# Long attention on one core: the key chunks of the first two query groups searched together

## The chip, the cores and the metric

The kernel runs on one core of one Trainium2 chip. The metric is the device time of one execution in microseconds (us); the figure for a kernel is the median over its runs.

## The reference, cut to what matters

The program is one long network over 2048 tokens of width 128. The order of its parts is a gated mixing block, two transformer layers with causal attention and experts (called `f` in the names of the trace), one attention without a mask (`b`), and the two transformer layers again (`g`). The change touches `b` alone:

```python
def _L0_attn_b_ref(x, Wq, bq, Wk, bk, Wv, bv, Wp):      # x: (1, 2048, 128)
    H, D = (16, 8)
    q = (x @ Wq + bq).reshape(Bb, Nn, H, D)
    ...
    q = jnp.einsum('bnhe,ei->bnhi', q, Wp)
    k = jnp.einsum('bnhe,ei->bnhi', k, Wp)
    scores = jnp.einsum('bnhi,bmhi->bnhm', q, k) / math.sqrt(D)
    attn = jax.nn.softmax(scores, axis=-1)
    out = jnp.einsum('bnhm,bmhe->bnhe', attn, v).reshape(Bb, Nn, E)
```

Every one of 2048 queries of 16 heads looks at all 2048 keys. The softmax is computed with the row maximum taken off first, and this maximum has to be found before the exponentials of a row can start.

## The kernel before, in words

**Tiling.** Tokens lie in 4 chunks (`CHUNKS`) of 512 and in 16 tiles of 128, 4 tiles to a chunk. Heads are taken 4 at a time (a quad). In `b` a *group* is one chunk of queries `c`, one quad and two of the chunk's four tiles, so 256 queries of 4 heads. There are 32 groups, in the order of `FULL_ORDER`: the 8 of query chunk 0 first. Groups 0 and 1 are the two halves of the same chunk and the same quad.

**Inputs.** Before `b`'s attention, `project_qkv` projects chunk by chunk. Queries and keys go out to DRAM in three bf16 parts and come back with another layout into `q_stack` and `k_stack`; each chunk of each stack is brought by DMAs of line 678, for the two halves of the partitions, on the SP, POOL and ACT queues. TensorE waits for a chunk of keys on its first use (`inputs("k", p)`).

**Search.** For each group, 16 *scans* (2 tiles, 2 pairs of heads, 4 chunks of keys) are searched: TensorE writes 128 queries times 512 keys of two heads into one of two buffers of `h_ps_scanb` (line 1393, two matmuls that run side by side), VectorE takes the maximum of 1024 columns (line 1545) and frees the buffer. `h_maxima_..b` holds the partial maxima, in two buffers by group number modulo 2. After a group's last scan VectorE reduces them to `h_row_maxb` (line 1564), TensorE turns that (`turn`, line 1413), VectorE negates it into `h_shiftsb` (line 1570), and SP sends it by DMA into a row of `q_stack` (line 1611), where it enters the scores as one more row of the product.

**Scores, exponentials, values.** For each group there are 16 *steps*, one per tile of keys. A step is one pair of score banks (line 1431, `h_ps_lowb` or `h_ps_highb`, a ring of 3), two exponentials on ScalarE (line 1497, `h_probsb`, a ring of 12), and 8 value matmuls (line 1452). After a group's last step ScalarE drains the result (`h_drainedb`, line 1506) and SP writes it out (line 1618).

**Order.** All three streams go through TensorE, which works in the order of its instructions. That order is fixed at build time by `Plan.orders()`: a loop that keeps modelled due times of each engine and picks the next of search, scores and values in turn, with some patience for the one whose turn it is. `Plan.searched` is the order of the search pieces. Two rules of the planner matter here: scores of a group may start only 4.2 us (`SHIFT`) after its turn, and a scan of group g may be placed only when the scoring has reached group g-2 (`x[1] - self.units[2 * n_pair][0] > 2` forbids it). The planner does not model the arrival of the key chunks. In `b` the search order is: the 16 scans of a group, tile by tile, pair by pair, and innermost the 4 chunks of keys; `turn` of a group stands behind the first scan of the next one.

After the last turn come the pieces `finish` (projection of the first three chunks of the result), placed in the same list.

Of the kernel before, what the change touches and what calls it, by code (L numbers as in the profile page):

```python
# [19 lines left out]
CHUNKS = S // CH  # L20
# [35 lines left out]
class Steps:  # L56


    def __init__(self, engine, sem, base=0):
        self.engine, self.sem, self.base, self.n = engine, sem, base, 0  # L60
# [973 lines left out]
SCALAR, SCALAR_NEXT, SCALAR_DONE = 0.833, 68.0, 222.0  # L1034
HIDE, SHIFT, WRITE = 85.0, 4200.0, 3000.0
INVERT, BIAS, SCALE, ADD, FINISH_COLUMNS = 450.0, 2200.0, 850.0, 1800.0, 4 * 650.0
INVERT_AFTER, GATHER, MOMENTS, KEEP = 5, 3500.0, 4500.0, 2200.0
CAUSAL_ORDER = [(c, n) for c, n in enumerate((TPC, TPC, 2, 2)) for _ in range(QUADS * TPC // n)]
FULL_ORDER = [(c, 2) for c in range(CHUNKS) for _ in range(QUADS * 2)]
# [4 lines left out]
class Plan:  # L1044
# [6 lines left out]
    def __init__(self, causal):  # L1051
        self.causal = causal
        if causal:
            chunks = CAUSAL_ORDER
        else:
            chunks = FULL_ORDER
        seen = [0] * CHUNKS
        self.groups = []
        for c, n in chunks:
            self.groups.append((c, seen[c] // TPC, seen[c] % TPC, n))  # L1060
            seen[c] += n
        assert seen == [QUADS * TPC] * CHUNKS
        self.blocks = [TPC * c + t0 + n if causal else TILES for c, _, t0, n in self.groups]
        self.searched = []
        for g, (c, _, t0, n) in enumerate(self.groups):
            pieces = [("scan", g, p, ((hp, t, SCAN_KEYS),)) for t in range(t0, t0 + n) for hp in range(2)
                      for p in range(c if causal else CHUNKS)]
            if causal:
                for hp in range(2):
                    pieces += [("scan", g, c, tuple((hp, t, (t + 1) * P) for t in ts)) for ts in self.together(g)]  # L1070
                if n == TPC:
                    pieces.append(("scan", g, c, ((0, 1, 2 * P), (1, 1, 2 * P))))
            self.searched += pieces[:1] + ([("turn", g - 1)] if g else []) + pieces[1:]
        self.searched.append(("turn", len(self.groups) - 1))
        self.searched += [("finish", c) for c in range(CHUNKS - 1)]
        if causal:
            self.searched += [("rows", c) for c in range(CHUNKS - 1)]
        self.ends = [max(g for g, x in enumerate(self.groups) if x[0] == c) for c in range(CHUNKS)]
        self.invert_at = {min(i for i, x in enumerate(self.searched) if x[:2] == ("scan", self.ends[c] + INVERT_AFTER)): c
                          for c in range(CHUNKS - 1)}  # L1080
        self.scale_at = self.searched.index(("finish", 0))
        self.turn_at = {x[1]: i for i, x in enumerate(self.searched) if x[0] == "turn"}
        self.end_of_search = {x[1]: i for i, x in enumerate(self.searched) if x[0] == "scan"}
        self.steps = [(g, kb) for g in range(len(self.groups)) for kb in range(self.blocks[g])]
        self.step_at = {x: n for n, x in enumerate(self.steps)}
        self.units = [(g, kb, k) for g, kb in self.steps for k in range(self.banks(g))]
        self.unit_at = {x: u for u, x in enumerate(self.units)}
        self.step_of = [self.step_at[x[0:2]] for x in self.units]
        self.exps = []
        for u, (g, kb, k) in enumerate(self.units):  # L1090
            self.exps.append(("exp", u))
            if g and (kb, k) == (0, self.banks(g) - 1):
                self.exps.append(("drain", g - 1))
        self.exps.append(("drain", len(self.groups) - 1))
        self.offsets = [max(0, kb - TPC * self.groups[g][0] - self.groups[g][2]) * P if causal else 0
                        for g, kb in self.steps]
        self.tensor, self.moves = self.orders()
# [1438 lines left out]
```

How the kernel before makes its waits and increments, by code:

```python
    def __call__(self, instruction):  # L62
        self.n += 1
        instruction.then_inc(self.sem, 1)
        self.engine.wait_ge(self.sem, self.base + self.n)
# [126 lines left out]
        @block.sync  # L192
# [16 lines left out]
                rest.append((m.w_att[:, :, i, :], ins["L0_ffn_" + name].rearrange("l p d -> p l d")))  # L209
            for i, name in enumerate(("Wq", "Wk", "Wv")):
                rest.append((m.w_b[:, i, :], ins["L0_attn_b_" + name]))
            for dst, name in ((m.bv[:, 0:LAYERS, :], "bv"), (m.bo[:, :, :], "bo"), (m.gate_b[:, :, :], "gate_b")):
                rest.append((dst, ins["L0_ffn_" + name].partition_broadcast(P)))
            rest.append((m.bv[:, LAYERS, :], ins["L0_attn_b_bv"].partition_broadcast(P)))
            rest.append((m.gate_w[:, :, :], ins["L0_ffn_gate_w"].rearrange("l p e -> p l e")))
            assert len(rest) == REST_LOADS
            for dst, src in rest:
                sp.dma_start(dst, src).then_inc(rest_in, 16)
            sp.wait_ge(rest_in, 16 * REST_LOADS)
            sp.wait_ge(x_in, 16)
# [1 line left out]
        @block.gpsimd  # L222
# [1 line left out]
            nc.gpsimd.memset(m.ident[:, :], 0.0).then_inc(built, 1)  # L224
            nc.gpsimd.memset(m.pick[:, :, :], 0.0).then_inc(built, 1)
            nc.gpsimd.memset(m.hide_right[:, :, :], 0.0).then_inc(built, 1)
            nc.gpsimd.memset(m.upto[:, :], 1.0).then_inc(built, 1)
            nc.gpsimd.memset(m.ones[:, :], 1.0).then_inc(built, 1)
            pool.wait_ge(built, 5)
            def select(t, op, fill, column, row, base=0):
```

## Time and profile before

| | us |
|---|---|
| median of 3 runs | 3134.47 (3134.13 to 3141.97) |
| profiled execution, its own time | 3133.52 |
| profiled execution, its span | 3131.5 |
| first scan of `b` (start) | 1316.6 |
| last drain of `b` (start) | 1975.0 |

The span is the stretch that the profiler saw; the time of the same execution is 2.0 us longer. Times in the rows are from the span's start. PE is the matrix engine, PEld its weight loads, DVE is VectorE, ACT ScalarE, POOL GpSimd, SP the queue of SyncE. "[1.03 <-PE x]" behind an instruction is the idle time of its engine just before it and what ended it. The granted clock (PEclk) is a share of 2.4 GHz: 1.00 is 2.4 GHz and 0.50 is 1.2 GHz.

### The profile page before, as it was taken

How to read it: one execution, taken by the hardware profiler on the slowest of the kernel's cores; microseconds unless marked ns; L12 is line 12 of the kernel's file. 1: busy time of each engine (PE TensorE's matmuls, PEld its weight loads, DVE VectorE, ACT ScalarE, POOL GpSimd, SP SyncE). 2: the span in 40 equal slices, each digit the busy share in tenths (PEclk: the TensorE clock that was granted, in tenths of full speed). 3: DMA queues.
4: the chain of work that ended last, by engine and by line, in shares of the span. 5: the costliest groups of instructions: out<-in, count | busy, mean ns of one | idle time of the engine just before them, and what ended most of it. 6: DMA issues, size and time to landing. Idle time of an engine off the chain costs nothing. (4 is left out here: it accounts for less than half of the span.)

```text
span 3131.5 us, 71460 instructions
## 1 busy us (share of the span) xinstructions
PE 2659.0 (85%) x28144; PEld 1161.8 (37%) x28144; DVE 2612.3 (83%) x3520; ACT 2248.4 (72%) x4330; POOL 608.7 (19%) x1145
## 2 busy tenths in 40 slices
PE   3569999899799995569999999489998998899976
PEld 3322333577323333312222223232333776323325
DVE  4569999787899995689999999389998887899976
ACT  1137988677489884349999998358887676688864
POOL 5233101444321011100000000132101443321011
PEclk8669999999899997879999999779999999899998
DMA  1061000215300000410000000330000215300001
GB/s 33 21 142 33 21 14 12 66 55 101 72 26 20 18 9 24 108 31 9 12 12 13 12 14 10 79 86 25 16 18 16 75 48 105 66 24 19 13 13 30
DMA packets 109882, 119.08 MB, mean 38 GB/s; under 512 B 20726, under 2 KB 87660, under 8 KB 109548
## 3 DMA queue, kind: packets, MB, share of 16 engines
q1 hardware_dynamic: 102444, 98.21, 12.0%
q0 software_dynamic: 4608, 13.96, 2.5%
q8 instruction: 222, 3.64, 0.5%
q10 hardware_dynamic: 2496, 2.36, 0.4%
q14 instruction: 112, 0.92, 0.1%
HBM read 70.31 MB, written 43.78 MB: 36 GB/s over the span
## 5 line engine op out<-in xcount | busy, mean ns | idle before, releaser
L1497 ACT ACTIVATE h_probsf<-h_ps_lowf 128x512 f32<-128x512 f32 (+3 forms) x812 | 424.3, 551 | 130.9 <-PE h_ps_lowf L1431 81.1
L1497 ACT ACTIVATE h_probsg<-h_ps_lowg 128x512 f32<-128x512 f32 (+3 forms) x812 | 424.3, 551 | 120.5 <-PE h_ps_lowg L1431 77.9
L1497 ACT ACTIVATE h_probsb<-h_ps_lowb 128x512 f32<-128x512 f32 x683 | 389.1, 596 | 78.6 <-PE h_ps_lowb L1431 60.4
L1452 PE MATMUL h_ps_valuesf<-h_probsf,v_all 128*9 128x256 f32 (+2 forms) x4608 | 353.6, 380 | 39.1 <-POOL h_probsf L1595 31.8
L1452 PE MATMUL h_ps_valuesg<-h_probsg,v_all 128*9 128x256 f32 (+2 forms) x4608 | 352.4, 378 | 30.3 <-POOL h_probsg L1595 22.9
L1452 PE MATMUL h_ps_valuesb<-h_probsb,v_all 128*9 128x256 f32 x4096 | 318.4, 383 | 9.3 <-ACT h_drainedb L1506 5.0
L1545 DVE TENSOR_REDUCE h_maxima_0b<-h_ps_scanb 128x2 f32<-128x1024 f32 x256 | 292.4, 1213 | 29.1 <-PE h_ps_scanb L1393 29.1
L1545 DVE TENSOR_REDUCE h_maxima_2b<-h_ps_scanb 128x2 f32<-128x1024 f32 x256 | 292.7, 1214 | 6.7 <-PE h_ps_scanb L1393 6.7
L1545 DVE TENSOR_REDUCE h_maxima_0f<-h_ps_scanf 128x2 f32<-128x1024 f32 x224 | 259.1, 1216 | 22.4 <-PE h_ps_scanf L1393 21.7
L1545 DVE TENSOR_REDUCE h_maxima_0g<-h_ps_scang 128x2 f32<-128x1024 f32 x224 | 258.9, 1215 | 19.8 <-PE h_ps_scang L1393 19.1
L1497 ACT ACTIVATE h_probsf<-h_ps_highf 128x512 f32<-128x512 f32 (+3 forms) x404 | 224.1, 555 | 37.2 <-PE h_ps_lowf L1431 34.6
L1497 ACT ACTIVATE h_probsg<-h_ps_highg 128x512 f32<-128x512 f32 (+3 forms) x404 | 224.1, 555 | 36.1 <-PE h_ps_lowg L1431 33.4
L1595 POOL TENSOR_SCALAR_AFFINE_SELECT h_probsg<-h_probsg 128x128 f32<-128x128 f32 (+1 forms) x384 | 125.6, 341 | 617.1 <-ACT h_probsg L1497 610.0
L1393 PE MATMUL h_ps_scanf<-k_stack,q_stack 48*128 48x512 bf16 (+3 forms) x1280 | 221.9, 367 | 26.6 <-issue 9.0
L1595 POOL TENSOR_SCALAR_AFFINE_SELECT h_probsf<-h_probsf 128x128 f32<-128x128 f32 (+1 forms) x384 | 124.9, 341 | 599.7 <-ACT h_probsf L1497 592.6
L1393 PE MATMUL h_ps_scang<-k_stack,q_stack 48*128 48x512 bf16 (+3 forms) x1280 | 219.1, 362 | 26.0 <-DVE h_maxima_0g L1545 7.7
L1431 PE MATMUL h_ps_lowf<-q_stack,k_stack 49*128 49x256 bf16 (+2 forms) x1368 | 229.6, 289 | 10.4 <-DMA q_stack<-h_shiftsf 4.5
L1431 PE MATMUL h_ps_lowg<-q_stack,k_stack 49*128 49x256 bf16 (+2 forms) x1368 | 227.7, 287 | 10.5 <-DMA q_stack<-h_shiftsg 4.3
L1393 PE MATMUL h_ps_scanb<-k_stack,q_stack 48*128 48x512 bf16 x1024 | 200.7, 389 | 39.6 <-DMA k_stack<-k_parts 25.5
L1497 ACT ACTIVATE h_probsb<-h_ps_highb 128x512 f32<-128x512 f32 x341 | 203.4, 596 | 18.6 <-PE h_ps_lowb L1431 15.5
L1431 PE MATMUL h_ps_lowb<-q_stack,k_stack 49*128 49x256 bf16 x1366 | 200.5, 275 | 10.3 <-ACT h_probsb L1497 10.1
L1545 DVE TENSOR_REDUCE h_maxima_2g<-h_ps_scang 128x2 f32<-128x1024 f32 x160 | 185.5, 1217 | 14.5 <-PE h_ps_scang L1393 13.5
(480 smaller groups left out, 5220.5 us busy)
## 6 DMA issues: line engine op xcount, KB each, us to landing
q_stack<-combine_weights SPq DMA_DIRECT2D x64, 256.0 KB, 3.6
q_stack<-in_L_ffn_e_w SPq DMA_DIRECT2D x24, 256.0 KB, 3.2
q_stack<-q_parts SPq DMA_DIRECT2D x22, 256.0 KB, 5.9
k_stack<-k_parts SPq DMA_DIRECT2D x22, 256.0 KB, 8.1
attended<-h_drainedf SPq DMA_DIRECT2D x16, 256.0 KB, 2.5
attended<-h_drainedf SPq DMA_DIRECT2D x32, 128.0 KB, 1.9
attended<-h_drainedb SPq DMA_DIRECT2D x32, 128.0 KB, 1.9
attended<-h_drainedg SPq DMA_DIRECT2D x16, 256.0 KB, 2.2
```

What stands on the lines that cost most here:

```text
L1393: last = nc.tensor.matmul(ps_scan[:, i % RING_A, b, at:at + width], m.q_stack[rows, c, 2 * quad + hp, t * P:(t + 1) * P], m.k_stack[rows, ...
L1431: last[b] = nc.tensor.matmul(ps_scores[(2 * n_pair + b) % RING_S][:, width * i + off:width * (i + 1)], m.k_stack[rows, kb // TPC, pair, at ...
L1452: last = nc.tensor.matmul(ps_values[32 * j:32 * j + VD, low:high], m.v_all[:, kb, QUAD * quad + j, :], probs[:, (u + j % banks) % RING_P, ...
L1497: nc.scalar.activation(by_head(probs[:, of % RING_P, :], of), by_head(ps_scores[of % RING_S], of), ACT.Exp, scale=SOFTMAX_SCALE).then_inc( ...
L1545: nc.vector.tensor_reduce(found[:, :, low], now, AXIS_X, ALU.max).then_inc(freed, 1)
L1595: nc.gpsimd.affine_select(out=at, in_=at, compare_op=ALU.is_ge, fill=0.0, base=0, pattern=[[0, at.shape[1]], [1, P]], channel_multiplier=- ...
```

## The change

The planner's order of search pieces is changed for the attention without a mask. The 32 scans of groups 0 and 1 form one list, sorted by chunk of keys: 4 scans of group 0 and 4 of group 1 with chunk 0, the same with chunk 1, chunk 2 and chunk 3. The turn of group 0 stands behind the first scan of group 1 with chunk 3, which is the 29th scan; the last three scans of group 1 follow. From group 2 on the order is the old one, so the turn of group 1 stands behind the first scan of group 2. Scans, turns, scores and values are the same in number and size; `orders()` is run on the new list, and so the interleaving of the three streams on TensorE follows from it.

```diff
+TOGETHER = 2
 ...
+            if not causal and g < TOGETHER:
+                first = sorted(first + pieces, key=lambda x: x[2]) if g else pieces
+                if g == TOGETHER - 1:
+                    at = next(i + 1 for i in range(len(first)) if first[i][1] == g and first[i][2] == CHUNKS - 1)
+                    self.searched += first[:at] + [("turn", 0)] + first[at:]
+                continue
             self.searched += pieces[:1] + ([("turn", g - 1)] if g else []) + pieces[1:]
```

## Rows read from the trace of the kernel before

**Rows 1.** The page: busy time, share of span and instructions of each engine.

```profile
span 3131.5 us, 71460 instructions
PE 2659.0 (85%) x28144; PEld 1161.8 (37%) x28144; DVE 2612.3 (83%) x3520; ACT 2248.4 (72%) x4330; POOL 608.7 (19%) x1145
```

**Rows 2.** Busy time by stretch of `b`: us, then PE, PEld, DVE, ACT, POOL, clock, DMA.

```profile
1316.00:1344.30 28.30, 2.20 (x10) 0.47 (x10) 3.85 (x4) 0.16 (x1) 4.40 (x8) 0.52 0.99 201
1344.30:1364.30 20.00, 10.35 (x39) 1.77 (x35) 19.39 (x19) 0.00 (x0) 0.00 (x0) 0.50 0.00 0
1364.30:1400.00 35.70, 34.69 (x398) 9.74 (x398) 33.75 (x33) 31.20 (x59) 0.00 (x0) 0.90 0.02 5
1400.00:1949.00 549.00, 525.30 (x6523) 155.25 (x6523) 538.74 (x525) 508.21 (x957) 0.00 (x0) 1.00 0.04 12
1949.00:1975.50 26.50, 22.90 (x269) 7.51 (x268) 6.76 (x19) 21.84 (x42) 0.00 (x0) 1.00 0.02 6
```

**Rows 3.** Timeline of DVE at the start of `b`: start, us, instruction, count.

```profile
1317.14 1.23 DVE L1545 TENSOR_REDUCE h_maxima_0b<-h_ps_scanb 128x2 f32<-128x1024 f32 x1 [0.97 <-PE h_ps_scanb L1393]
1323.67 1.23 DVE L1545 TENSOR_REDUCE h_maxima_0b<-h_ps_scanb 128x2 f32<-128x1024 f32 x1 [5.31 <-PE h_ps_scanb L1393]
1336.35 1.23 DVE L1545 TENSOR_REDUCE h_maxima_0b<-h_ps_scanb 128x2 f32<-128x1024 f32 x1 [11.45 <-PE h_ps_scanb L1393]
1344.35 14.80 DVE L1545 TENSOR_REDUCE h_maxima_0b<-h_ps_scanb 128x2 f32<-128x1024 f32 x13 [6.78 <-PE h_ps_scanb L1393]
1359.18 0.19 DVE L1564 TENSOR_REDUCE h_row_maxb<-h_maxima_0b 128x8 f32<-128x32 f32 x1
1359.29 1.22 DVE L1545 TENSOR_REDUCE h_maxima_2b<-h_ps_scanb 128x2 f32<-128x1024 f32 x1
1360.42 0.27 DVE L1570 TENSOR_SCALAR h_shiftsb<-h_ps_scanb 8x128 bf16<-8x128 f32 x1
1361.21 6.88 DVE L1545 TENSOR_REDUCE h_maxima_2b<-h_ps_scanb 128x2 f32<-128x1024 f32 x6 [0.53 <-PE h_ps_scanb L1393]
...
1372.12 8.01 DVE L1545 TENSOR_REDUCE h_maxima_2b<-h_ps_scanb 128x2 f32<-128x1024 f32 x7 [0.35 <-PE h_ps_scanb L1393]
1380.16 0.19 DVE L1564 TENSOR_REDUCE h_row_maxb<-h_maxima_2b 128x8 f32<-128x32 f32 x1
```

**Rows 4.** Who waited for whom from 1316 to 1344.35: total, times, longest.

```profile
PE h_ps_scanb L1393 <- DMA k_stack<-k_parts: 25.5, 3, 12.1
```

**Rows 5.** Timeline of ACT and PE where the first scores start.

```profile
1364.94 1.09 ACT L1497 ACTIVATE h_probsb<-h_ps_lowb 128x512 f32<-128x512 f32 x2 [48.78 <-PE h_ps_lowb L1431]
...
1364.30 0.61 PE L1431 MATMUL h_ps_lowb<-q_stack,k_stack 49*128 49x256 bf16 x4
...
1368.49 1.04 PE L1452 MATMUL h_ps_valuesb<-h_probsb,v_all 128*9 128x256 f32 x8
...
1370.43 1.04 PE L1452 MATMUL h_ps_valuesb<-h_probsb,v_all 128*9 128x256 f32 x8
...
1373.09 0.62 PE L1452 MATMUL h_ps_valuesb<-h_probsb,v_all 128*9 128x256 f32 x8
...
1374.18 0.62 PE L1452 MATMUL h_ps_valuesb<-h_probsb,v_all 128*9 128x256 f32 x8
```

**Rows 6.** Timeline around one change of group in the middle of `b`.

```profile
1706.32 0.39 PE L1393 MATMUL h_ps_scanb<-k_stack,q_stack 48*128 48x512 bf16 x2
1706.80 0.12 PEld L1452 LDWEIGHTS h_ps_valuesb<-h_probsb,v_all 128*9 128x9 f32 x8 [0.38 <-ACT h_probsb L1497]
1706.80 0.62 PE L1452 MATMUL h_ps_valuesb<-h_probsb,v_all 128*9 128x256 f32 x8
1707.35 0.11 PEld L1431 LDWEIGHTS h_ps_lowb<-q_stack,k_stack 49*128 49x128 bf16 x4 [0.43 <-DMA q_stack<-h_shiftsb]
...
1707.78 1.08 ACT L1497 ACTIVATE h_probsb<-h_ps_lowb 128x512 f32<-128x512 f32 x2 [1.03 <-PE h_ps_lowb L1431]
...
1708.43 0.28 PE L1431 MATMUL h_ps_highb<-q_stack,k_stack 49*128 49x256 bf16 x1 [0.47 <-ACT h_probsb L1497]
...
1708.75 0.39 ACT L1506 ACTIVATE h_drainedb<-h_ps_valuesb 128x256 f32<-128x256 f32 x1
1709.01 0.62 ACT L1497 ACTIVATE h_probsb<-h_ps_highb 128x512 f32<-128x512 f32 x1
```

**Rows 7.** Timeline of the end of `b`'s attention: last row maxima, last drain.

```profile
1948.43 0.19 DVE L1564 TENSOR_REDUCE h_row_maxb<-h_maxima_2b 128x8 f32<-128x32 f32 x1
...
1975.01 0.38 ACT L1506 ACTIVATE h_drainedb<-h_ps_valuesb 128x256 f32<-128x256 f32 x1 [0.74 <-PE h_ps_valuesb L1452]
```

## The prediction

> **What bounds the kernel now.** I read the busy shares first [rows 1]: no engine is full over the whole span, so the answer must come from the stage that the change touches. The chain of work that ended last goes back only to 1990.8 us and never reaches `b`'s attention, so it says nothing here. I therefore cut `b` into stretches [rows 2]. Four regimes are to be seen. From 1316 to 1344.3 every engine is idle (VectorE 3.85 us busy of 28.3) while the DMA engines are at 0.99: the stage waits for the key chunks. From 1344.3 to 1364.3 only the search runs, with VectorE at 19.39 of 20.00 us. From 1400 to 1949 all three engines are close to full, VectorE the fullest: 538.74 of 549.00 us, 98.1%, against 95.7% of TensorE and 92.6% of ScalarE. The last 26.5 us belong to the scores of the last group.
>
> The start in detail [rows 3]: VectorE does one scan of each key chunk at 1317.14, 1323.67, 1336.35 and 1344.35, with idle gaps of 5.31, 11.45 and 6.78 us before the last three, 23.54 us together. The waits name the cause: TensorE waited three times, 25.5 us in all, for DMAs of `k_stack` [rows 4]. After the fourth chunk has landed, 13 reductions run in 14.80 us. With one reduction alone at 1.23 us that is (14.80 - 1.23) / 12 = 1.131 us per scan.
>
> In the middle, one group takes VectorE (1948.43 - 1380.16) / 30 = 18.94 us from one row maximum to the next [rows 3, 7]: 16 scans are 18.1, the rest is the row maximum, the shift and the small gap at the turn. ScalarE and TensorE need less for a group's scores. A step takes 1.09 us (from 1373.09 to 1374.18 between two value blocks [rows 5]), so 16 steps are 17.44 us, and the drain adds 0.26 (from 1708.75 to 1709.01 [rows 6]): 17.7. The missing 1.2 us is visible once per group: TensorE does a scan and values at 1706.32 and 1706.80 with no scores between, ScalarE idles 1.03 us, and the scores start when the DMA of the shifts has landed [rows 6]. So before, the scores of every group wait for the search of that group, and the search is paced by VectorE. That is the path which sets the end of the stage; what is saved on VectorE ahead of the last turn is saved at the end, if nothing else takes over.
>
> **The change, part by part.** *Removed:* the idle time at the chunks. Eight scans need each chunk instead of one. Starting at 1317.14, VectorE is done with the 8 scans of chunk 0 at 1317.14 + 9.05 = 1326.2, after the first use of chunk 1 was possible (1323.67). The 16th is over at 1335.2; chunk 2 can be reduced at 1336.35, so 1.1 us of idle time stays. The 24th is over at 1345.4, after chunk 3 (1344.35), so no gap. Recovered: 23.54 - 1.1 = 22.4 us. The projections and the DMA issues ahead do not depend on the scans, so I keep the landing times.
>
> *Moved:* the row maximum of group 0 comes after 28 scans: 1336.35 + 12 x 1.131 + 0.1 = 1350.0, where before it came at 1359.18. One scan later stands its turn, at 1351.3. From the shift at 1360.42 to the first scores at 1364.30 there were 3.9 us [rows 3, 5], so the scores start at about 1355.2, 9.1 us earlier. The row maximum of group 1 comes at about 1355.6 instead of 1380.16, 24.5 us earlier. Behind each of these stand the same instructions as before: one turn on TensorE, one shift on VectorE, the DMAs of line 1611 on SP, with no wait in front of them on SP, since the first write of a result comes a whole group later. No instruction is added; the sort costs nothing on the chip.
>
> *The clock.* Scans alone do not bring TensorE to 2.4 GHz here: from 1344.3 to 1364.3 they ran at a granted 0.50, that is 1.2 GHz [rows 2], and steps took 1.94 us (1368.49 to 1370.43) until 1371.5, 7.2 us after the first scores [rows 5]. In that time VectorE lost about 1.9 us: 15 scans of group 1 took 18.92 us from 1361.21 to 1380.13 where 15 x 1.131 + 0.1 = 17.1 were due [rows 3]. I take the same loss in the new kernel, now in group 2: the 24.5 us are then 22.6, in keeping with the 22.4 above. The Trainium skill, page "TensorE: Matmul & The Clock Gate", Part 1, holds that the throttled clock is the default and that activity releases it; as the new kernel has no long gap on TensorE after 1317, that rule leaves room for a clock that stays up, while the rows here show 20 us of just such scans at 1.2 GHz. By the row the sum stays 22.4; by the rule the 1.9 us would come on top, 24.3.
>
> *The streams after that.* Now group 0 and group 1 are both searched when the first scores start, and the scores have a stock. Scores of group 1 could start at 1356.7 + 3.9 = 1360.6, and are reached only after 16 steps from 1355.2, with four of them slow: 1355.2 + 16 x 1.13 + 4 x 0.8 = 1376.5. So the scoring is 16 us behind what the search would allow, and the scores of a group no longer wait. They gain 18.94 - 17.7 = 1.2 us per group, and have caught up after 13 groups or so; with 31 to go, the last groups wait for their search as before, and the tail from the last row maximum to the last drain (1948.43 to 1975.39, 27 us [rows 7]) is unchanged. In code the same count shows: the search has 17 pieces per group (16 scans and the turn), the scores have 16, and a strict rotation lets them gain one step per group.
>
> *What this costs:* (a) the rule of two groups ahead. The first scan of group 3 may be placed only when the scores of group 1 have begun. The search is 50 pieces in at that point, the scores begin at about piece 33 and need 16: just met or missed by one round. Between 0 and 1.1 us (one scan), I take 0.5. For later groups the search loses one place per group against that bound, and it is met. (b) While the scores catch up, 17 steps fall on one group of search. ScalarE then needs 17 x 1.09 + 0.26 = 18.8 us of 18.94, so three engines run with almost no slack over rings of 2 and 3 buffers. No row of before shows this. From below: 0, as the engines fit. From above: TensorE's wait for ScalarE at a change of group, 0.47 us [rows 6], passed on to VectorE in each of 14 groups, 6.6 us. I take 0.5, near the lower end, since VectorE ran on through the same 0.47 us waits in the middle of `b`.
>
> *Sum:* 22.4 - 0.5 - 0.5 = 21.4 us. The profiled execution took 3133.52 us (span 3131.5), so 3112.1; the median of the runs shown is 1.0 us higher, so the forecast is 3113. After `b` all stages start earlier by the same amount and have the same work.
>
> **The rivals.** *The scores become the bound (gain 9).* They start only 9.1 us earlier. If in the crowded rotation a group of scores still takes 18.94 us, because TensorE's order or ScalarE's drain holds it, then they never catch up, and the stage ends 9.1 us earlier: 3125.4. For it: ScalarE would be 99% busy. Against it: the steps of 1.09 us in rows 5 ran with a scan in each of them. Its first mark is that the scores still trail by 10 us or more at the last group. Chance 0.09.
>
> *The clock stays at 2.4 GHz (gain 24).* The scans keep it up from 1317, and the slow rounds vanish: 21.4 + 1.9 = 23.3, up to 24.3 without the two costs; 3110 to 3111. Against it stand the 20 us at 0.50. Chance 0.09.
>
> *The change does not do what it says (no gain).* The scans now read `k_stack` while DMAs write other chunks of it, at a DMA share of 0.99. If those land later, the gain shrinks by the delay of chunk 3 beyond 1345.4; with 22 us of delay it is gone, 3134. No row speaks for it: the stretches show no reads beside these writes. Chance 0.04.
>
> *Slower: the clock stays at 1.2 GHz in the crowded part.* A round of scan, scores and values takes 1.94 us at 1.2 GHz against VectorE's 1.131, so each slow round costs 0.81 us. Before, four of them passed until the clock rose. If it rose later now, the 21.4 us would be used up by 26 more slow rounds, and with 38 more the kernel would be 9.4 us slower, 3144. Against it: in before the clock rose while just such rounds ran. Chance 0.03.
>
> **How the numbers follow.** The forecast case has 0.75. Its own range is 3112 to 3120: a gain of 22.4 without the two costs, and of 22.4 - 6.6 - 1.1 = 14.7 with both at their upper bounds. The range that is to hold 8 times in 10 takes in the clock rival at 24.3 with the 1.1 us gap at chunk 2 closed too (3109, and 1 for the spread of the dates that I read off), and above the part of the first rival in which the scores catch up only partly: 3108 to 3124. A measurement of this kernel can tell about 0.3%, 9.4 us, from no change. Faster by more than that: the forecast and the clock rival, 0.84, and half of the first rival, 0.88 in all. Within 0.3%: the other half and the case without effect, 0.09. Slower: 0.03.
>
> **What the profile after would show.** Reductions of line 1545 from 1317 on with one gap near 1335 of about 1 us and no other above 0.6 us until 1350. First row maximum at 1350 and the second at 1355.6; first exponential at 1355.8. No idle time of ScalarE at the change of group up to group 12 or 14, and 1.03 us after that. The last row maximum near 1927, last drain near 1954, then every stage as before. I am wrong if chunk 3 lands after 1346, if VectorE shows idle time at each group between 1360 and 1600, or if the scores are not held by the search at group 31.

## The result, and the profile after

The changed kernel takes 3114.29 us (median of 4 runs, 3109.95 to 3115.89), the kernel before 3136.37 us (median of 4, 3134.13 to 3141.97: the three runs shown ahead and one of 3138.27). The ratio is 0.9932, 95% interval 0.9919 to 0.9945. The forecast was 3113 us in a range of 3108 to 3124.

First the page of the changed kernel, to be read against [rows 1]: the busy times agree within 4 us, the span is 20.0 us shorter. The work is the same; waiting has gone.

```profile
span 3111.5 us, 71460 instructions
PE 2657.7 (85%) x28144; PEld 1162.9 (37%) x28144; DVE 2616.2 (84%) x3520; ACT 2248.7 (72%) x4330; POOL 610.5 (20%) x1145
```

Then the busy times by stretch of `b` after the change, with the columns of [rows 2]:

```profile
1316.00:1344.30 28.30, 12.58 (x44) 2.26 (x44) 26.62 (x26) 3.06 (x5) 6.33 (x12) 0.59 1.05 223
1344.30:1355.00 10.70, 5.62 (x19) 1.05 (x19) 10.14 (x12) 0.00 (x0) 0.00 (x0) 0.50 0.04 7
1355.00:1400.00 45.00, 42.98 (x491) 12.13 (x489) 42.06 (x42) 38.48 (x73) 0.00 (x0) 0.89 0.02 7
1400.00:1927.00 527.00, 510.74 (x6381) 151.78 (x6379) 517.66 (x503) 498.60 (x939) 0.00 (x0) 1.00 0.04 12
```

In the first stretch VectorE is busy 26.62 us of 28.3, where it was 3.85; some 3 of the 26.62 us are projections that stood ahead of 1316 before. The timeline of VectorE shows how, against [rows 3]:

```profile
1320.31 4.62 DVE L1552 TENSOR_REDUCE h_maxima_0b<-h_ps_scanb 128x2 f32<-128x1024 f32 x4 [0.97 <-PE h_ps_scanb L1400]
1324.84 4.61 DVE L1552 TENSOR_REDUCE h_maxima_2b<-h_ps_scanb 128x2 f32<-128x1024 f32 x4
1329.37 4.61 DVE L1552 TENSOR_REDUCE h_maxima_0b<-h_ps_scanb 128x2 f32<-128x1024 f32 x4
1333.89 4.61 DVE L1552 TENSOR_REDUCE h_maxima_2b<-h_ps_scanb 128x2 f32<-128x1024 f32 x4
1338.94 4.62 DVE L1552 TENSOR_REDUCE h_maxima_0b<-h_ps_scanb 128x2 f32<-128x1024 f32 x4 [0.44 <-PE h_ps_scanb L1400]
...
1352.64 0.19 DVE L1571 TENSOR_REDUCE h_row_maxb<-h_maxima_0b 128x8 f32<-128x32 f32 x1
...
1358.18 0.19 DVE L1571 TENSOR_REDUCE h_row_maxb<-h_maxima_2b 128x8 f32<-128x32 f32 x1
...
1362.15 1.23 DVE L1552 TENSOR_REDUCE h_maxima_0b<-h_ps_scanb 128x2 f32<-128x1024 f32 x1 [0.71 <-PE h_ps_scanb L1400]
...
1379.40 0.19 DVE L1571 TENSOR_REDUCE h_row_maxb<-h_maxima_0b 128x8 f32<-128x32 f32 x1
...
1928.86 0.19 DVE L1571 TENSOR_REDUCE h_row_maxb<-h_maxima_2b 128x8 f32<-128x32 f32 x1
```

Four reductions of one group and four of the other alternate, with one gap of 0.44 us at chunk 2 where before 23.54 us were idle. In this execution the first reduction stood at 1320.31, before at 1317.14. Dates of two executions are therefore compared from here on from the first reduction of line 1545 (1552 after). *The stage* means the time from there to the start of the last drain.

| row maximum of group | before | after | earlier by |
|---|---|---|---|
| 0 | 42.0 | 32.3 | 9.7 |
| 1 | 63.0 | 37.9 | 25.1 |
| 2 | 81.9 | 59.1 | 22.8 |
| 12 | 271.3 | 248.6 | 22.7 |
| 31 | 631.3 | 608.5 | 22.7 |
| last drain (the stage) | 657.9 | 635.1 | 22.7 |

The lead of 25.1 us at group 1 loses 2.3 us in group 2, at the slow clock (0.50 up to 1365.2), and then stays to a tenth of a microsecond over 29 groups.

The timeline of ScalarE shows where the scores run into the search again. The last three drains of the catching up and the first group that waits, against [rows 6]:

```profile
1539.83 0.39 ACT L1513 ACTIVATE h_drainedb<-h_ps_valuesb 128x256 f32<-128x256 f32 x1
1558.05 0.39 ACT L1513 ACTIVATE h_drainedb<-h_ps_valuesb 128x256 f32<-128x256 f32 x1
1575.85 0.39 ACT L1513 ACTIVATE h_drainedb<-h_ps_valuesb 128x256 f32<-128x256 f32 x1
1593.69 0.60 ACT L1504 ACTIVATE h_probsb<-h_ps_highb 128x512 f32<-128x512 f32 x1 [1.03 <-PE h_ps_lowb L1438]
1612.59 0.60 ACT L1504 ACTIVATE h_probsb<-h_ps_lowb 128x512 f32<-128x512 f32 x1 [1.03 <-PE h_ps_highb L1438]
```

Between the first drain at 1379.61 and the gap at 1593.69 no group starts with the wait of 1.03 us, and the drains follow at 17.8 us (once 18.2). From group 13 on the wait is there every 18.9 us, as in the kernel before.

The 20.0 us of the spans are put together thus: the stage 22.7 shorter, the part behind it 0.4 shorter (1156.5 to 1156.1 us from the last drain to the end), the part ahead of it 3.2 longer. Of the last, 2.2 us are there already at the last scan of `f` (1157.7 before, 1159.9 after), in code that the change does not touch; the runs of one kernel differ by as much.

### The profile page after: what moved, and what is told of

It reads as the page before. It is cut to its first block and busy times, and to the rows that moved or that the text cites. A ratio compares the mean times of both kernels' runs of the same rounds, so it can differ in the third digit from the quotient of the medians.

```text
span 3111.5 us, 71460 instructions
## 1 busy us (share of the span) xinstructions
PE 2657.7 (85%) x28144; PEld 1162.9 (37%) x28144; DVE 2616.2 (84%) x3520; ACT 2248.7 (72%) x4330; POOL 610.5 (20%) x1145
## 5 line engine op out<-in xcount | busy, mean ns | idle before, releaser
L1552 DVE TENSOR_REDUCE h_maxima_0f<-h_ps_scanf 128x2 f32<-128x1024 f32 x224 | 259.4, 1217 | 22.1 <-PE h_ps_scanf L1400 21.4
L1552 DVE TENSOR_REDUCE h_maxima_0g<-h_ps_scang 128x2 f32<-128x1024 f32 x224 | 258.8, 1216 | 19.3 <-PE h_ps_scang L1400 18.6
L1400 PE MATMUL h_ps_scanb<-k_stack,q_stack 48*128 48x512 bf16 x1024 | 202.8, 393 | 22.4 <-DVE h_maxima_0b L1552 9.8
L1552 DVE TENSOR_REDUCE h_maxima_2g<-h_ps_scang 128x2 f32<-128x1024 f32 x160 | 185.5, 1218 | 14.4 <-PE h_ps_scang L1400 13.5
```

What stands on the lines that cost most here:

```text
L1400: last = nc.tensor.matmul(ps_scan[:, i % RING_A, b, at:at + width], m.q_stack[rows, c, 2 * quad + hp, t * P:(t + 1) * P], m.k_stack[rows, ...
L1552: nc.vector.tensor_reduce(found[:, :, low], now, AXIS_X, ALU.max).then_inc(freed, 1)
```

## The experiments

Every kernel was compared with the kernel before on the same chip. The ratio of medians is given first, then the stage from its profile, which is the finer measure here: it does not contain what the rest of the program moves from one execution to the next (the first reduction of the stage stood anywhere from 1315.5 to 1322.3). It is still read from one execution of each kernel, and two things in it move by themselves: the gap at chunk 2 was 0.44, 0.94, 1.31, 1.74 and 2.03 us in five kernels with the same work ahead of it, and the granted clock rose between 5.0 and 8.0 us after the first scores in the kernels without added matmuls. So a difference of a microsecond or two between two stages says nothing of an edit unless a row shows where it arises. "Theory A" is that of the prediction: the search sets the end, so what VectorE idles less at the chunks is gained. "Theory B": the gain goes with the start of the first scores.

**Only one group sorted.**

```diff
+            if not causal and g == 0:
+                pieces = sorted(pieces, key=lambda x: x[2])
             self.searched += pieces[:1] + ([("turn", g - 1)] if g else []) + pieces[1:]
```

> Only group 0's own 16 scans are sorted by chunk of keys (4 per chunk); group 1 and its turn stand as before. Measured inside the stage, from the start of its first reduction to the start of its last drain, before is 657.9 us and the change 635.1. Theory A (the gain is the idle time of VectorE at the chunks, wherever the first scores start): 4 scans are 4.6 us, so VectorE idles about 2.0 us before chunk 1, 8.1 before chunk 2 and 3.4 before chunk 3, 13.5 instead of 23.5: stage 647.9, program 10 us faster than before, with first scores 10.3 us earlier. Theory B (the gain goes with the start of the first scores, which the change brought some 9 us forward): the first scores start as early as in the change, so the stage should be as short as the change's, 635 to 638.

Measured: ratio 0.9964 (0.9951 to 0.9978), 3124.28 us; the stage 1970.1 - 1322.3 = 647.8 us, 10.1 less than before. Timeline of VectorE in this kernel:

```profile
1322.32 4.62 DVE L1547 TENSOR_REDUCE h_maxima_0b<-h_ps_scanb 128x2 f32<-128x1024 f32 x4 [0.92 <-PE h_ps_scanb L1395]
1328.62 4.62 DVE L1547 TENSOR_REDUCE h_maxima_0b<-h_ps_scanb 128x2 f32<-128x1024 f32 x4 [1.69 <-PE h_ps_scanb L1395]
1341.05 4.62 DVE L1547 TENSOR_REDUCE h_maxima_0b<-h_ps_scanb 128x2 f32<-128x1024 f32 x4 [7.80 <-PE h_ps_scanb L1395]
1349.36 4.62 DVE L1547 TENSOR_REDUCE h_maxima_0b<-h_ps_scanb 128x2 f32<-128x1024 f32 x4 [3.70 <-PE h_ps_scanb L1395]
```

The gaps add up to 13.2 us (13.5 expected), and the stage is A's to 0.1 us. The first exponential starts 37.4 us after the first reduction, in the change 38.1. So the same start of the scores gives 10 us here and 23 there: theory B is out.

**The turn of group 0 eleven scans later (behind the 40th instead of the 29th), without and with room.** Both kernels keep the 32 sorted scans in one piece and have this:

```diff
-                    self.searched += first[:at] + [("turn", 0)] + first[at:]
+                    self.searched += first
                 continue
+            if not causal and g == TOGETHER:
+                self.searched += pieces[:8] + [("turn", 0), ("turn", 1)] + pieces[8:]
+                continue
```

The second has one line more:

```diff
-            if x[0] == "scan" and n_pair < len(self.units) // 2 and x[1] - self.units[2 * n_pair][0] > 2:
+            if x[0] == "scan" and n_pair < len(self.units) // 2 and x[1] - self.units[2 * n_pair][0] > (2 if self.causal else 3):
```

> The change, but the turn of group 0 is moved from the 29th scan to behind the 40th (8 scans of group 2), right ahead of the turn of group 1. First scores start some 12 us later; the search of groups 0 and 1 is as in the change. Theory A with the planner's rule of two groups ahead: the scan list may go on to group 3 only when the scores have reached group 1; that is now 11 rounds late, so VectorE idles about 11 x 1.09 = 12 us once, before group 3, and the stage is 647 us, 12 more than the change. Theory B: 12 us more as well, but without idle time of VectorE before group 3.

> As the kernel with the late turn, and in the attention without a mask the search may be three groups ahead of the scores instead of two. Theory A (VectorE's stream sets the end, and the scores, 1.16 us per group faster than the search, catch up from a lag of 16 + 12 = 28 us in some 24 of 31 groups): no idle time before group 3, stage 635 us as the change, though the first scores start 12 us later than there and later than 1364, the time of before. Theory B: 12 us more than the change, 647.

Measured: 0.9960 (0.9946 to 0.9974) and a stage of 647.4 us without room; 0.9934 (0.9920 to 0.9947) and 635.6 us with it. The row that tells them apart, after the row maximum of group 2, in the timeline of VectorE without room:

```profile
1374.18 0.18 DVE L1574 TENSOR_REDUCE h_row_maxb<-h_maxima_0b 128x8 f32<-128x32 f32 x1
1386.49 1.23 DVE L1555 TENSOR_REDUCE h_maxima_2b<-h_ps_scanb 128x2 f32<-128x1024 f32 x1 [12.13 <-PE h_ps_scanb L1403]
```

and the same place with room:

```profile
1377.74 0.19 DVE L1574 TENSOR_REDUCE h_row_maxb<-h_maxima_0b 128x8 f32<-128x32 f32 x1
1378.32 1.23 DVE L1555 TENSOR_REDUCE h_maxima_2b<-h_ps_scanb 128x2 f32<-128x1024 f32 x1 [0.39 <-PE h_ps_scanb L1403]
```

In both the first exponential starts 51.3 to 51.7 us after the first reduction, 13 us later than in the change and later than before (47.8). With room the stage is 0.4 us longer, and the gap at chunk 2 alone was 0.5 us longer than in the change (0.94 instead of 0.44): the scores have that much slack. Without room the planner's rule holds back the first scan of group 3 until the scores reach group 1, and VectorE idles 12.13 us once. This is the rule of term (a) of the prediction, missed by eleven rounds here; in the change itself it was met, with no gap at group 3.

**No wait for any later chunk.** In the old order the scans of groups 0 and 1 all read key chunk 0 (3 of 4 chunks are left out of these maxima):

```diff
+                if not causal and g < 2:
+                    p = 0
                 inputs("k", p)
```

> The old order of the search, but all scans of groups 0 and 1 read key chunk 0, so that no scan waits for a later chunk. It leaves out 3 of 4 chunks from these two groups' maxima; number and size of the instructions are unchanged. This is the most that any order of the search can recover. Theory A: idle time of 23.5 us gone, stage 657.9 - 23.5 = 634.4 us, only 0.5 to 1 us less than the change. Theory B: first scores start near 1340, 24 us earlier than before and 15 earlier than in the change, so the stage would be 10 us or more below the change's, 620 to 625.

Measured: 0.9933 (0.9920 to 0.9947), stage 637.7 us. Neither number was met: 3.3 us more than A's bound, and 2.6 us more than the change. Timelines of VectorE and TensorE around the first scores in this kernel:

```profile
1340.18 0.27 DVE L1572 TENSOR_SCALAR h_shiftsb<-h_ps_scanb 8x128 bf16<-8x128 f32 x1
...
1348.50 2.52 DVE L1547 TENSOR_REDUCE h_maxima_2b<-h_ps_scanb 128x2 f32<-128x1024 f32 x2 [2.91 <-PE h_ps_scanb L1395]
...
1343.39 0.61 PE L1395 MATMUL h_ps_scanb<-k_stack,q_stack 48*128 48x512 bf16 x2 [0.53 <-DVE h_maxima_2b L1547]
1347.42 0.61 PE L1433 MATMUL h_ps_lowb<-q_stack,k_stack 49*128 49x256 bf16 x4 [3.43 <-DMA q_stack<-h_shiftsb]
```

And stretches of it, with the columns of [rows 2]:

```profile
1339.00:1343.00 4.00, 2.01 (x7) 0.40 (x7) 3.48 (x5) 0.00 (x0) 0.00 (x0) 0.50 1.08 215
1343.00:1347.40 4.40, 0.61 (x2) 0.10 (x2) 2.59 (x3) 0.00 (x0) 0.00 (x0) 0.50 0.71 95
...
1346.00:1346.50 0.50, 0.00 (x0) 0.00 (x0) 0.00 (x0) 0.00 (x0) 0.00 (x0) 0.50 0.17 23
1346.50:1347.00 0.50, 0.00 (x0) 0.00 (x0) 0.00 (x0) 0.00 (x0) 0.00 (x0) 0.50 0.03 6
```

All 16 scans of group 0 ran through without a gap (18.19 us), and its shift was started at 1340.18, while the DMAs still brought the later chunks (a DMA share of 1.08 from 1339 to 1343 and 0.71 up to 1347.4). The four DMAs of 0.5 KB that carry the shifts then let the scores start only 7.2 us after the shift, against 3.9 before [rows 3, 5]. SP issued the four in 2.55 us, before in 2.54, so the rest of the delay lies behind the issue. The traffic of the loads ends at about 1346.4, 1.0 us ahead of the scores: with no scan waiting for a later chunk, the scores still started close behind the end of the loads, as the first scan of chunk 3 does in the kernel before. The edit thus took away the waits of the scans, but it was no bound for the whole start. TensorE stood in front of these scores for 3.43 us, the scans behind them in its order waited too, and VectorE idled 2.91 us. Searching group 0 first is thus worth nothing here even where its keys are there: the change, which has the shifts ready behind the loads, is 2.6 us better than this "bound".

**VectorE's pace taken away.** Both kernels, before and changed, with reductions over half of the columns from group 2 on (half of the keys left out of these maxima):

```diff
+                        if not causal and g >= 2:
+                            now = now[:, :, 0:SCAN_KEYS // 2]
                         nc.vector.tensor_reduce(found[:, :, low], now, AXIS_X, ALU.max).then_inc(freed, 1)
```

> The kernel before, with VectorE's reductions from group 2 on over half of the columns (256 of 512 keys a head); the maxima of these groups leave out half of the keys. VectorE then needs about 0.6 us per scan instead of 1.13 and cannot set the pace any more; TensorE's and ScalarE's 17.7 to 17.9 us per group do. Stage (first reduction to last drain) about 657.9 - 30 x 1.1 = 625 us. Alone it says nothing; it is the reference for its partner with the change.

> The change with the same halved reductions from group 2 on. Theory A (the 22.7 us stay to the end because VectorE is the pace of the stage; the scores alone started only 9.7 us earlier): with VectorE out of the way the stage ends by the scores, so the change is worth 9.7 us plus the scans that TensorE has done ahead, 12 x 0.31 = 3.7, so 10 to 14 us against its partner. Theory C (the idle time recovered at the chunks comes back at the end, whatever sets the pace later): 22 to 23 us against its partner.

Measured: before with light reductions 0.9983 (0.9974 to 0.9992), stage 648.7 us; changed with light reductions 0.9913 (0.9900 to 0.9927), stage 629.7 us. The difference of 19.0 us is neither A's 10 to 14 nor C's 22 to 23, but it is nearer to C, and the first kernel did not come near its 625 us. Two rows of VectorE in the first, one group apart:

```profile
1715.98 0.18 DVE L1566 TENSOR_REDUCE h_row_maxb<-h_maxima_2b 128x8 f32<-128x32 f32 x1
...
1734.67 0.18 DVE L1566 TENSOR_REDUCE h_row_maxb<-h_maxima_0b 128x8 f32<-128x32 f32 x1
```

A group takes 18.69 us although VectorE is now idle over a third of the time (185.97 us busy of the 300 from 1600 on). The prediction's "TensorE and ScalarE need 17.7" holds only for groups that lie searched in stock. When the scores wait for their search, the order of TensorE has one round per group with a scan and values and no scores, and 17 rounds of 1.09 us are 18.5 (the other 0.2 us were not followed). So VectorE's 18.94 us is the pace of the stage by 0.25 us only; right below it lies the written order.

The 3.7 us that the change is worth less here (22.7 - 19.0) can be followed group by group. The lead of the row maxima is 22.1 us at group 1, 20.8 at group 2, 19.0 at group 13, and 19.1 from there to the end. So 3.0 of the 3.7 us are missing at group 1 already, ahead of the first lighter reduction, and have nothing to do with VectorE's pace. The gap at chunk 2 shows most of it:

```profile
1336.44 4.62 DVE L1554 TENSOR_REDUCE h_maxima_0b<-h_ps_scanb 128x2 f32<-128x1024 f32 x4 [2.03 <-PE h_ps_scanb L1400]
```

It is 2.03 us here, 0.44 in the change, and the partner had 22.9 us of gaps instead of 23.5: the idle time recovered in this pair is 20.9 us, and its lead at group 2 is 20.8. (The rest of the 3.0 us is the partner's clock, which rose 2.0 us sooner after the first scores than in the kernel before, so that its group 1 was 0.8 us shorter.) From group 2 to group 13 another 1.8 us go. While the scores have a stock, a group of search takes 18.82 us in the changed kernel, against 18.69 without a stock:

```profile
1450.46 0.18 DVE L1573 TENSOR_REDUCE h_row_maxb<-h_maxima_0b 128x8 f32<-128x32 f32 x1
...
1469.27 0.18 DVE L1573 TENSOR_REDUCE h_row_maxb<-h_maxima_2b 128x8 f32<-128x32 f32 x1
```

This is the crowded rotation of term (b). In the real kernel the same crowding disappears under VectorE's 18.94. Theory C, less the crowding, is what this pair shows.

**The same pair with an order written for a fast VectorE.**

```diff
-                    freed.append(vector + VECTOR_DONE + VECTOR * 2 * width)
-                    vector += VECTOR_NEXT + VECTOR * 2 * width
+                    read = width if not self.causal and x[1] >= 2 else 2 * width
+                    freed.append(vector + VECTOR_DONE + VECTOR * read)
+                    vector += VECTOR_NEXT + VECTOR * read
```

> The kernel before with the halved reductions from group 2 on (half of the keys left out of these maxima), and now the planner's cost of such a reduction is halved too, so that the order on TensorE is written for a fast VectorE. In the run with the old order a group took 18.68 us although VectorE was idle a third of the time: one round without scores stood in the order of each group. Theory D (that round is the floor of the old order, and the scores alone need 17.75): groups now take 17.8 us, the stage 47.5 + 32 x 17.8 + 3 slow rounds = 620 us, 28 less than with the old order (648.7).

> The change, with the halved reductions from group 2 on and with their planned cost halved. Theory D: with both VectorE and the written order out of the way the end is set by the scores alone, and the change is worth only what the first scores start earlier, 7.5 to 9.7 us against its partner: stage 611 to 613 us. If the recovered idle time of VectorE counts by itself (theory C), 19 to 22 us against its partner.

Measured: 0.9937 (0.9925 to 0.9950), stage 636.6 us, and 0.9878 (0.9864 to 0.9892), stage 618.0 us: 18.5 us apart. Theory D is wrong in both. The changed kernel shows the dense pace while its stock lasts (17.85 us per group up to group 11):

```profile
1410.34 0.18 DVE L1574 TENSOR_REDUCE h_row_maxb<-h_maxima_0b 128x8 f32<-128x32 f32 x1
...
1428.19 0.18 DVE L1574 TENSOR_REDUCE h_row_maxb<-h_maxima_2b 128x8 f32<-128x32 f32 x1
```

The other never gets it: eight groups from the drain at 1405.57 to that at 1552.23 take 18.33 us each. Cheaper planned reductions don't let the search run ahead; the planner's code offers a reason, since its rotation still gives the search about one place per round, and it has 17 pieces to 16 steps. In the changed kernel too the scores wait for their search again, from group 23 on in every second group. So with a fast VectorE the end was still set by where the search stands. The lead of the row maxima is not constant in this pair, 19.8 us at group 2, 24.9 at group 10 and 17.6 at group 31, so that its 18.5 us are a result and no proof that the idle time of the start comes back one for one. Why the rounds without scores come back in some groups and not in others there (17.6 and 18.8 us in turn) was not followed.

**TensorE kept busier ahead of the scores.** A second pair of bf16 matmuls behind each of the first 32 scans, and in another kernel a float32 matmul:

```diff
+                if not causal and g < TOGETHER:
+                    hp, t, width = parts[0]
+                    for b, bank in enumerate((ps_high[:, :], ps_low[:, 1, :])):
+                        rows = slice(HALF * b, HALF * b + STACK)
+                        last = nc.tensor.matmul(bank, m.q_stack[rows, c, 2 * quad + hp, t * P:(t + 1) * P],
+                                                m.k_stack[rows, p, 2 * quad + hp, 0:width], start=True, stop=True)
```

```diff
+                if not causal and g < TOGETHER:
+                    last = nc.tensor.matmul(ps_high[:, 0:P], m.ident[:, :], m.ident[:, :], start=True, stop=True)
```

> The change, with a second pair of 512-column matmuls behind each of the first 32 scans (the results go to score banks that are not read before they are written anew). Tests the clock term: in the change the first four rounds of scores still ran at 1.2 GHz and VectorE idled 0.71 + 0.71 + 0.38 us. If more activity of TensorE ahead of the scores raises the clock, these idle gaps vanish, the first rounds take 1.09 us and the stage is 633.3 us, 1.8 less than the change (635.1). If not, it is 635 us or, where the added 0.43 us per scan at 1.2 GHz makes TensorE late for VectorE, some us more.

> The change, with one float32 matmul of 128 x 128 by 128 columns behind each of the first 32 scans (its result is never used). The pair of bf16 matmuls on 48 rows per scan left the clock at 0.50 with TensorE over 80% busy, and it rose only 7 us after the first float32 value matmuls. If it is this kind of work that raises it, the granted clock is 1.00 when the scores begin, the gaps of 0.71 us vanish and the stage is 1.8 us shorter than the change's 635.1. If not, it stays at 635 to 637.

Measured: 0.9942 (0.9929 to 0.9956), stage 637.9 us; 0.9957 (0.9944 to 0.9970), stage 641.6 us. Both stages are longer than the change's, by 2.8 and 6.5 us, mainly since TensorE now comes late for VectorE: four reductions take 4.72 us with the bf16 pair instead of 4.62, and with float32 there are gaps of 0.16 to 0.30 us at every second scan. (0.6 of the 2.8 us are a longer gap at chunk 2.) The clock did not rise. Stretches of the kernel with the bf16 pair, and below them of that with float32:

```profile
1322.00:1340.00 18.00, 14.70 (x58) 2.03 (x56) 16.86 (x15) 0.00 (x0) 4.40 (x8) 0.50 1.08 228
1362.00:1366.00 4.00, 4.00 (x32) 0.81 (x28) 2.58 (x3) 2.17 (x4) 0.00 (x0) 0.50 0.00 1
```

```profile
1322.00:1340.00 18.00, 17.45 (x56) 8.21 (x56) 16.36 (x15) 0.00 (x0) 4.42 (x8) 0.50 1.09 231
1366.00:1370.00 4.00, 4.00 (x32) 0.82 (x28) 2.57 (x3) 1.98 (x5) 0.00 (x0) 0.50 0.00 1
```

With float32 TensorE is shown busy for 17.45 of 18 us and the granted clock is still 0.50; in both it is 0.50 in the first rounds of scores too. It rose 7.3 us after the first scores before the change, 7.4 after it, 8.8 with the bf16 pair and 8.5 with float32; but in the ten other kernels, none of which has more matmuls, it was between 5.0 and 8.0 us, and 5.3 us in the kernel before with light reductions, whose work is the same up to there. What raises it stays open.

**The clearing of the value bank beside the first scan.** TensorE waits for `cleared` ahead of the first values only:

```diff
-                pe.wait_ge(cleared, 1)
+                if causal:
+                    pe.wait_ge(cleared, 1)
 ...
+                    if (g, kb) == (0, 0) and not causal:
+                        pe.wait_ge(cleared, 1)
```

> The change, and TensorE waits for the clearing of the value bank only ahead of the first value matmuls instead of ahead of the first scan. Now VectorE's MEMSET (0.48 us) and the first scan (0.97 us of idle time of VectorE) follow one another; side by side the first reduction can start about 0.5 us earlier after the last instruction of the projection. From then on nothing changes: stage 635.1 us, the time from the end of the projection to the first reduction 1.0 instead of 1.5 us. If the first scan waits for its key chunk instead, no difference.

Measured: 0.9933 (0.9919 to 0.9947), 3112.26 us. The first reduction now follows the clearing at once, 0.5 us after the last instruction of the projection instead of 1.6. But the chunk was not there earlier:

```profile
1340.40 4.62 DVE L1555 TENSOR_REDUCE h_maxima_0b<-h_ps_scanb 128x2 f32<-128x1024 f32 x4 [3.27 <-PE h_ps_scanb L1400]
```

The gap there is 3.27 us instead of 0.44 and the stage 637.0. The 1.1 us gained ahead are lost at the chunk, and chunk 2 could be reduced 1.7 us later here, counted from the end of the projection (21.9 us instead of 20.2). No row ties that second part to the edit. With two groups together, the arrival of chunk 2 is the next bound at the start.

**Three groups together.** The list of 48 scans, partial maxima in buffers by `g // 2 % 2`, the search up to three groups ahead:

```diff
-TOGETHER = 2
+TOGETHER = 3
 ...
+                    for done in range(g):
+                        at = next(i + 1 for i in range(len(first)) if first[i][1:3] == (done + 1, CHUNKS - 1))
+                        first.insert(at, ("turn", done))
+                    self.searched += first
```

> Three groups searched together, 12 scans per chunk of keys, turns of groups 0 and 1 inside chunk 3; the partial maxima alternate buffers by pair of groups and the search may be three groups ahead. 24 scans of chunks 0 and 1 take 27 us, so that chunk 2, which came 0.4 to 3.3 us too late in the runs so far, is in time. First scores some 14 us later than in the change. Theory A: stage 634 to 635 us, 0.4 to 1 less than the change; nothing that the time can tell. Theory B (start of the first scores): 649.

Measured: 0.9935 (0.9922 to 0.9948), 3112.71 us, stage 1955.2 - 1319.7 = 635.5 us. No gap at any chunk is left on VectorE, as expected, but the 0.44 us that this gives are spent again: from the first row maximum to that of group 3 there are six gaps of 0.37 to 0.76 us, the slow rounds among them. It ties with the change; B's 649 us is refuted once more. No kernel with the full computation beat the change by more than a measurement can tell.

## Why the prediction was right

- *Recovered idle time, 22.4 us.* Right. 23.54 us of gaps became 0.44 in the profiled execution; 1.1 had been forecast. The gap at chunk 2 was 0.44 to 2.03 us in the five kernels that reach it alike, so this was luck to within about 1 us.
- *Dates.* The row maxima of groups 0 and 1 were forecast 32.9 and 38.5 us after the first reduction (1350.0 and 1355.6) and came at 32.3 and 37.9. The lead at group 1 was 25.1 us (24.5 forecast), at group 2 22.8 (22.6).
- *The clock.* Right by the row, not by the other reading: scans alone ran at 0.50 from 1324 on, and the first rounds of scores took 1.94 us again (value blocks at 1360.10, 1362.04, 1363.98). That the slow rounds cost nearly the same as before (2.3 us against 1.9 forecast) was partly luck, since the clock rose between 5.0 and 8.0 us after the first scores in kernels without added matmuls. The rule of the Trainium skill ("TensorE: Matmul & The Clock Gate", Part 1), that the throttled clock is the default and activity releases it, was no guide to when that happens here: added matmuls, up to a busy share of 97% in the rows, left it at 0.50. The rival with the clock at 2.4 GHz is refuted, and so is that with a clock that stays down (3144): it rose at 1365.2.
- *Cost (a), the rule of two groups ahead.* Taken at 0.5, was 0. That the rule acts is shown by the late turn: 12.13 us for a turn eleven scans later.
- *Cost (b), the crowded rotation.* Taken at 0.5, was below 0.1: the lead goes from 22.8 at group 2 to 22.7 at group 13. The light pair shows that it exists (18.82 against 18.69 us per group); in the real kernel it fits below VectorE's 18.94.
- *The scores catch up.* Forecast at "13 groups or so"; the first wait of 1.03 us is at group 13.
- *The unchanged tail.* 27 us forecast; 26.6 us from the last row maximum to the last drain before (1948.43 to the start at 1975.01) and 26.6 after (1928.86 to 1955.44).
- *The sum.* 21.4 us forecast, 22.7 in the stage, 22.1 between the medians, 0.68% by the ratio. The gaps recovered were 0.7 us more than forecast and the two costs of 0.5 us were not there; the slow rounds took back 0.4. That 3113 and the measured 3114.29 lie 1.3 us apart is two errors of opposite sign: the forecast started from 3134.5 for the kernel before, whose median came out at 3136.37, 1.9 us higher, and the gain between the medians was 0.7 larger.

The reasoning had one flaw that the number did not show: what paces a group. "ScalarE and TensorE need less, 17.7 us" was read as room below VectorE's 18.94 in every group. The light kernels show that a group whose scores wait for its search takes 18.69 us in the written order with reductions of 0.69 us too. The gain was not tied to VectorE's pace: with VectorE out of the way it was still 19.0 and 18.5 us. The path is the stream of the search, whatever paces it. A reason lies in the count that the prediction made for the scores only: the search has 17 pieces to 16 steps in one rotation, so what it is behind it cannot make up. The light runs fit this; none of them changes the count by itself.

The rivals: the scores as bound (3125.4) is refuted by the late turn with room, which started them later than before and lost 0.4 us. Chunks landing later under the new reads did not show: chunk 2 was reducible 18.6 us after the first reduction (19.2 before). Chunk 3 made nobody wait, so its landing can't be read.

## What to carry to other kernels

Where inputs arrive in pieces and the first consumer needs all of them, let the first consumers share each piece; what counts is not how early the first result is there but how far the stream that sets the end has got when the last piece has landed. Compare the dates of that stream group by group between two traces, from a common start: a lead that stays constant to the end shows that this stream carries it, and the place where it changes shows the cost. It does not show which engine paces the stream: the lead was as constant at 19.1 us where VectorE was idle over a third of the time. A fixed order of instructions is a bound of its own: with reductions of 0.69 instead of 1.23 us on the busiest engine the stage moved by 1.4%, and by another 1.9% when the order was written anew for them.

## What the runs showed of the hardware

- TensorE stayed at a granted 0.50 (1.2 GHz) for some 40 us of scans with float32 matmuls between them, at 17.45 us busy of 18.00, and was at 1.2 GHz still in the first rounds of scores, as it was in all other kernels. The clock rose 5.0 to 8.0 us after the first scores without added matmuls, and 8.8 and 8.5 us after them with added ones.
- Four DMAs of 0.5 KB issued while the loads of the key chunks were under way let the scores start 7.2 us after the shift instead of 3.9, at DMA shares of 1.08 and 0.71 meanwhile, and 1.0 us after the traffic of the loads had ended. This was seen in one run.
